# A linear-attention block on one core: the closing's second norm as u*r + w, the last projection in column halves, another order of the closing

## Chip, cores, metric

One core of one Trainium2 chip. The metric is the device time of one execution in microseconds; the median of several executions is compared. "Span" is the time from the first to the last instruction in the profiled execution.

## What is computed

For x of 2 x 4096 x 512 (float32), cut to what the kernel computes:

```python
norm(t) = (t - mean(t)) / sqrt(var(t) + 1e-5)             # over the 512 columns
ffn(t)  = norm(t) * ln_g + ln_b      # what the reference's feed-forward part leaves here
x = x + 0.5 * ffn(norm(x))
x = x + attn(norm(x))
x = x + 0.5 * ffn(norm(x))

def attn(x):                         # 16 heads of 32
    q, k = elu(x @ Wq.T) + 1, elu(x @ Wk.T) + 1
    v = x @ Wv.T
    # for each token t: S += k_t v_t^T ; z += k_t ; out_t = (q_t S) / (q_t . z + 1e-5)
    return out @ Wo.T + bo
```

The kernel writes the two norms of a half step as a gain 1 + rstd * ln_g/2 on x - mean, plus mean, plus ln_b/2. The second half step is what this change touches: with X2 the attention's residual sum, m and r its mean and reciprocal deviation, it is (X2 - m) * (1 + r * gain) + m + shift, where `gain` and `shift` hold half of ln_g and ln_b.

## The kernel before

The 4096 tokens are cut into 32 chunks of 128, and each chunk holds two tiles (batch 0 and 1) of 128 x 512. Weights are turned once at the start and kept as float16 high and low halves; every product of a projection is three passes (high by high, high by low, low by high) over four blocks of 128, so a projection of one tile is 12 matmuls of 512 columns.

Each engine has its own hand-written list of steps, `opening`, `body` and `closing`. The body runs two chunks each time and is software-pipelined: `now` and `prev` are `ops(Step)` objects whose steps act on chunk s (attention), s+1 (projection), s+2 (first norm) and s-1 (`back`, second norm and store). After the loop, `closing` writes out the steps of the last chunks as straight code: `fourth` is chunk 29, `third` 30, `second` 31 and `last` 32, whose `back` steps finish chunk 31. The order between engines comes from semaphores only; within an engine the list's order holds, and a step that waits holds all steps behind it. SyncE issues the transposing transfers (`turn_x`, `turn_k`, `turn_q`, `turn_attn`) in the order of its list.

The steps that the prediction follows, by engine:

- TensorE: `scores` (L1628, the scores of four heads of a chunk into SC), `attend` (L1651, into AV), `update` (L1678, the running state), `project_q`, `project_k`, `project_v` (matmuls at L1595 into PJ), `project_out` (L1690, matmuls at L1700, into PJ).
- VectorE: `mask` (L1165), `split_a` (L1175), `reciprocals` (L1219), `quotient` (L1232), `attn_low` (L1251), `add_out` (L1262: X2 = PJ * out_scale + X1BO), `out_stats` (L1271), `out_mean` (L1282), `back_gain` (L1289: TP = (X2 - m) * TP), `back_y` (L1311: Y = TP + m + shift), and for the last tile of all `back_gain_part` (L1296) and `back_y_part` (L1302) on halves of the columns.
- ScalarE: `copy_scores` (L769), `sums` (L801), `attn_half` (L809), `back_scale` (L700: TP = 1 + r * gain), `back_scale_part` (L667), `store_y` (L660), `store_tile`, `store_part` (L672 and L676).
- GpSimd: `x1_bias` (L432: X1BO = X1 + bo, both tiles), `rstd2_of_x2` (L470 and L472: r for both tiles), `rstd2_of_tile` (L478 and L480), `split_a` (L499), `spread_k`, `spread_q` (L507, L514), `split_s` (L522).
- SyncE: `turn_k` (L309), `turn_q` (L324), `turn_attn` (L335).

At the end of the closing the second norm of a tile therefore goes VectorE (X2, statistics, mean), GpSimd (r), ScalarE (1 + r * gain), VectorE (product, sum), and a store.

## Time and profile before

| | us |
|---|---|
| median of 3 executions | 926.44 (926.18 to 927.87) |
| the profiled execution | 925.02 |
| its span | 923.3 |
| TensorE busy | 892.6 (97%) |
| VectorE busy | 831.2 (90%) |
| ScalarE busy | 754.6 (82%) |
| GpSimd busy | 705.7 (76%) |

Busy times are of the profiled execution. PE is TensorE's matmuls, PEld its weight loads, DVE VectorE, ACT ScalarE, POOL GpSimd, SP SyncE; a q behind a name is the engine's queue of issued transfers. The granted clock of TensorE was 0.996 of full over the span. In a timeline, successive instructions of one kind are merged into one row (x2 is two of them), and matmul rows carry a modelled end, so rows of one engine can overlap by some tenths of a microsecond.

### The profile page before, as it was taken

The page shows a single profiled execution, that of the slowest core. Times are in us where ns is not written, and L with a number is a line of the kernel's source. Part 1 is how long each engine was busy: PE and PEld are TensorE (multiplying, and loading weights), DVE is VectorE, ACT ScalarE, POOL GpSimd, SP SyncE. Part 2 cuts the span into 40 slices and gives each one's busy share as a digit, 9 for nine tenths or more (in the row PEclk, how much of TensorE's full clock was granted, in tenths as well). Part 3 has the DMA queues.
Part 4 walks back from the last instruction along what each step waited for, and adds up shares of the span by engine and source line. Part 5 has one row for each costly group of instructions (what it writes and reads, how often), then busy time and mean ns, then how long its engine had stood idle before and what let it go on. Part 6 is the DMA issues. An engine that isn't in the chain of part 4 may idle for free.

```text
span 923.3 us, 30249 instructions
## 1 busy us (share of the span) xinstructions
PE 892.6 (97%) x10252; PEld 524.5 (57%) x10252; DVE 831.2 (90%) x1537; ACT 754.6 (82%) x1301; POOL 705.7 (76%) x869
## 2 busy tenths in 40 slices
PE   3999999999999999999999999999999999999985
PEld 3555556656555655555665555665555565655562
DVE  7889889999999999999999999999999999999787
ACT  6888888888888888888888888888888888888772
POOL 3369777779777778877778877778977777987772
PEclk9999999999999999999999999999999999999998
DMA  7586797666677766678766668766667766667873
GB/s 250 137 155 131 146 179 159 144 142 150 146 167 159 156 139 148 151 155 165 162 136 153 146 146 182 158 139 146 149 146 171 159 153 142 148 147 160 160 114 94
DMA packets 422090, 140.62 MB, mean 152 GB/s; under 512 B 402608, under 2 KB 402864, under 8 KB 422064
## 3 DMA queue, kind: packets, MB, share of 16 engines
...
q8 instruction: 15, 0.25, 0.1%
q14 instruction: 11, 0.09, 0.1%
...
## 4 chain that ended last, share of the span: by engine, by line
PE 90%; DVE 3%; DMA 2%; issue 2%; SPq 1%; POOL 1%; ACT 1%; DVEq 0%; ACTq 0%; POOLq 0%
PE PJ L1595 51%; PE PJ L1700 16%; PE AV L1674 8%; PE SC L1647 6%; PE AV L1686 5%; PE AV L1671 3%; DMA X<-in_L_attn_x_dram 1%; DMA KS<-KN 1%; SPq L324 1%; DVE AM L1165 0%; DMA AT<-ATTN 0%; PE SC L1572 0%; POOL A L499 0%; DVE TP L1289 0%; DVE wT L1079 0%
## 5 line engine op out<-in xcount | busy, mean ns | idle before, releaser
L1595 PE MATMUL PJ<-wT,XT 128*128 128x512 f16 x2304 | 523.9, 379 | 0.2
L1595 PEld LDWEIGHTS PJ<-wT,XT 128*128 128x128 f16 x2304 | 217.1, 98 | 243.5 <-issue 1.9
L499 POOL TENSOR_TENSOR A<-AM,A 128x512 f16<-128x512 f32 x252 | 288.2, 1163 | 29.1 <-ACT A L782 28.8
L1700 PE MATMUL PJ<-wT,AT 128*128 128x512 f16 x768 | 175.9, 379 | 1.0 <-DMA AT<-ATTN 0.9
L489 POOL TENSOR_SCALAR_AFFINE_SELECT AM<-AM 128x512 f32<-128x512 f32 x124 | 79.2, 639 | 112.9 <-ACT AM L769 112.9
L782 ACT ACTIVATE A<-AM 128x512 f16<-128x512 f32 x256 | 153.9, 632 | 13.9 <-POOL AM L489 10.1
L1674 PE MATMUL AV<-VN,A 128*128 128x33 f16 x3072 | 116.3, 177 | 0.0
L1700 PEld LDWEIGHTS PJ<-wT,AT 128*128 128x128 f16 x768 | 71.2, 97 | 78.1 <-DMA AT<-ATTN 2.1
L1671 PE MATMUL AV<-SS,QS 128*128 128x33 f16 x1024 | 111.7, 178 | 0.0
L1674 PEld LDWEIGHTS AV<-VN,A 128*128 128x128 f16 x3072 | 108.8, 96 | 3.7
L1165 DVE TENSOR_TENSOR AM<-SC,causal 128x512 f32<-128x512 f32 x132 | 90.0, 685 | 19.0 <-PE SC L1647 18.8
L1671 PEld LDWEIGHTS AV<-SS,QS 128*128 128x128 f16 x1024 | 98.0, 96 | 4.0 <-POOL A L499 0.3
L769 ACT ACTIVATE AM<-SC 128x512 f32<-128x512 f32 x124 | 74.1, 598 | 21.8 <-PE SC L1647 21.6
L1647 PE MATMUL SC<-QS,KS 96*128 96x128 f16 x1024 | 83.5, 219 | 4.1 <-issue 2.3
L1647 PEld LDWEIGHTS SC<-QS,KS 96*128 96x128 f16 x1024 | 67.6, 97 | 33.2 <-issue 2.5
L727 ACT ACTIVATE PHI<-PJ,inv_scale 128x512 f32<-128x512 f32 x64 | 43.7, 682 | 44.6 <-PE PJ L1595 44.5
L507 POOL COPY KN<-KN 128x1024 f16<-128x1024 f16 x64 | 66.7, 1043 | 12.5 <-ACT KN L757 12.5
L432 POOL TENSOR_TENSOR X1BO<-X,obias 128x1024 f32<-128x1024 f32 x32 | 75.5, 2359 | 0.0
L522 POOL TENSOR_TENSOR SS<-S,SC_HI 128x528 f16<-128x528 f32 x62 | 73.7, 1189 | 2.0 <-ACT SC_HI L817 1.9
L747 ACT ACTIVATE QN<-PJ,f_scale 128x1024 f16<-128x1024 f32 x64 | 72.1, 1126 | 0.7 <-DVE PJ L1181 0.7
L1125 DVE SCALAR_TENSOR_TENSOR X<-TP,stat,shift 128x512 f32<-128x512 f32 x64 | 47.8, 748 | 19.4 <-POOL X1BO L432 19.3
L1686 PEld LDWEIGHTS AV<-VN,KN 128*128 128x128 f16 x1984 | 58.1, 96 | 7.8 <-DVE TP L1232 0.2
...
## 6 DMA issues: line engine op xcount, KB each, us to landing
...
XT<-XH SPq DMA_TRANSPOSE x64, 3.3
...
```

Source lines behind the costliest of these rows:

```text
L432: g.tensor_tensor(X1BO[:, st.parity(1)], X1[:], obias[:].unsqueeze(1).to_broadcast([P, BATCH, E]), ALU.add).then_inc(x1bo_done.sem, 1)
L489: g.affine_select(out=am, in_=am, compare_op=ALU.is_ge, fill=0.0, base=0, pattern=[[0, QUADS], [1, C]], channel_multiplier=-1).then_inc(sc ...
L499: g.tensor_tensor(A[:, b, LO, hg], AM[:, k % 4], A[:, b, HI, hg], ALU.subtract).then_inc(a_lo.sem, 1)
L769: a.activation(AM[:, k % 4], SC[hg % 2][:], ACT.Copy, scale=SUM_DOWN).then_inc(sc_copied.sem, 1)
L782: a.activation(A[:, b, HI, hg], AM[:, k % 4], ACT.Copy).then_inc(a_hi.sem, 1)
L1165: v.tensor_tensor(AM[:, k % 4].rearrange("p (h q) -> p h q", h=QUADS), SC[hg % 2][:].rearrange("p (h q) -> p h q", h=QUADS), causal[:].uns ...
L1595: ins = t_.matmul(PJ[b], XT[:, w, c, b * C:(b + 1) * C], wT[m_][:, m, c, :], start=(c, w, m) == todo[0], stop=(c, w, m) == todo[-1])
L1647: ins = t_.matmul(SC[hg % 2][:, h * C:(h + 1) * C], KS[cur][0:STACK, head, b * C:(b + 1) * C], QS[cur][0:STACK, head, b * C:(b + 1) * C], ...
L1671: t_.matmul(to, QS[cur][:, head, b * C:(b + 1) * C], SS[:, b, hf, j * DA:(j + 1) * DA], start=True, stop=False)
L1674: ins = t_.matmul(to, A[:, b, w, hg, h * C:(h + 1) * C], VN[cur][:, b, m, head, :], start=False, stop=(w, m) == PASSES[-1])
L1686: ins = t_.matmul(AV2[:, hf, j * DA:(j + 1) * DA], stack, VN[cur][:, b, m, head, :], start=m == HI, stop=m == LO)
L1700: ins = t_.matmul(PJ[b], AT[:, b, w, c * C:(c + 1) * C], wT[3][:, m, c, :], start=(c, w, m) == todo[0], stop=(c, w, m) == todo[-1])
```

## The change

Only code outside the loop's path changes. For chunks 30 and 31 the second half step is computed as u*r + w, with u = (X2 - m) * gain (`gain_u`, VectorE, into TP, reading `gain` from SBUF) and w = X2 + shift. u and r no longer depend on each other. For tiles 0 and 1 of chunk 30 and tile 0 of chunk 31, w is made by GpSimd (`x2_shift`), u*r by ScalarE (`scale_u`), their sum by GpSimd (`sum_y`), and SyncE stores the tile (`store_tile`). For tile 1 of chunk 31, w is made from the projection directly: GpSimd adds shift to X1BO (`x1bo_shift`), VectorE adds the projection (`make_w`, two halves), VectorE makes u*r + w in one instruction (`last_y`), and ScalarE stores the tile whole (`store_last`). r is computed for each tile alone (`rstd2_of_tile`). The last projection, of tile 1 of chunk 31, is done in two halves of 256 columns, the first into PJ[1], the second into SC[0] (`project_out_part`), with its addition and statistics in halves too (`add_out_part`, `out_stats_part`). The parts of the last tile in `back_scale_part`, `back_gain_part`, `back_y_part` and `store_part` are gone.

The order of the closing changes on all engines but SyncE, where only the three stores are added. Left out of the diff below: a new small tile and the new semaphores, conditions in `back_scale` that are no longer needed, and more swaps of neighbouring steps. Of these, ScalarE begins with `sums(0)`, `q_half(0)`, `copy_scores(1, 3)`, `back_scale(1)` of chunk 29 in place of `back_scale(1)`, `copy_scores(1, 3)`, `sums(0)`, `q_half(0)`, and takes `third.copy_scores(1, 3)` ahead of `third.split_a(1, 0)`; VectorE takes `fourth.reciprocals(0)` ahead of `back_y(0)`, `add_s(0)` ahead of `back_gain(1)`, `phi_q(1)` ahead of `back_y(1)`, `low_k(1)` ahead of `low_v(0)`, and for chunk 30 `add_s(0)` ahead of `attn_low(0)` and `quotient(1)` ahead of `second.split_a(0, 1)`; TensorE takes `second.attend(0, 0)` ahead of `second.scores(1, 1)`. The indentation is cut by 16.

```diff
@@ -382,6 +392,9 @@
 second.turn_attn(1)
+second.store_tile(0)
+second.store_tile(1)
+last.store_tile(0)
 
...
@@ -471,13 +484,33 @@
 
+    def x2_shift(b):
+        pool.wait_ge(*x_gained.upto(back, b))
+        pool.wait_ge(*x2_done.upto(back, b))
+        g.tensor_tensor(X[:, st.parity(-1), b], X2[:, b], shift[:], ALU.add).then_inc(x2_shifted.sem, 1)
+
+    def x1bo_shift():
+        pool.wait_ge(*x_gained.upto(s, 1))
+        pool.wait_ge(*x1bo_done.upto(s))
+        g.tensor_tensor(X[:, st.parity(0), 1], X1BO[:, st.parity(0), 1], shift[:], ALU.add).then_inc(x1bo_shifted, 1)
+
     def rstd2_of_tile(b):
-        if b == 0 and st.has(-2):
+        end = back - (steps - 2)
+        if ATTEND:
             pool.wait_ge(*g2_done.upto(st.chunk(-2), 1))
+        else:
+            pool.wait_ge(*u_scaled.upto(0, b))
         pool.wait_ge(*stat2_done.upto(back, b))
-        g.tensor_scalar(var2[:, b:b + 1], stat2[:, b, 1:2], 1.0 + EPS, EPS * EPS, ALU.mult, ALU.add).then_inc(var2_done.sem, 1)
-        pool.wait_ge(*var2_done.upto(back, b))
-        g.tensor_tensor(rstd2[:, b:b + 1], var2[:, b:b + 1], neg_half[:, b:b + 1], ALU.pow).then_inc(rstd2_done.sem, 1)
+        g.tensor_scalar(var2[:, b:b + 1], stat2[:, b, 1:2], 1.0 + EPS, EPS * EPS, ALU.mult, ALU.add).then_inc(var2_tile.sem, 1)
+        pool.wait_ge(*var2_tile.upto(end, b))
+        g.tensor_tensor(rstd2[:, b:b + 1], var2[:, b:b + 1], neg_half[:, b:b + 1], ALU.pow).then_inc(rstd2_tile.sem, 1)
+
+    def sum_y(b):
+        end = back - (steps - 2)
+        pool.wait_ge(*u_scaled.upto(end, b))
+        pool.wait_ge(*x2_shifted.upto(end, b))
+        to = (Y if ATTEND else X1)[:, b]
+        g.tensor_tensor(to, to, X[:, st.parity(-1), b], ALU.add).then_inc(y_summed.sem, 1)
 
...
@@ -576,23 +609,23 @@
 fourth, third, second, last = ops(Step(0, steps - 3)), ops(Step(0, steps - 2)), ops(Step(0, steps - 1)), ops(Step(0, steps))
+fourth.spread_q(0)
 fourth.cut(1, 3)
-fourth.spread_q(0)
 fourth.split_a(1, 1)
...
 fourth.spread_k(1)
+fourth.split_s(0)
 fourth.spread_q(1)
 third.split_a(0, 0)
-fourth.split_s(0)
 third.cut(0, 3)
-fourth.split_s(1)
 third.rstd2_of_x2()
...
 third.split_a(0, 3)
+fourth.split_s(1)
 third.spread_k(0)
...
@@ -609,10 +642,18 @@
 second.split_a(1, 2)
-second.rstd2_of_x2()
 third.x1_bias()
+second.x1bo_shift()
+second.x2_shift(0)
+second.rstd2_of_tile(0)
+second.x2_shift(1)
+second.rstd2_of_tile(1)
+last.x2_shift(0)
+second.sum_y(0)
+second.sum_y(1)
 last.rstd2_of_tile(0)
 last.rstd2_of_tile(1)
+last.sum_y(0)
 
...
@@ -659,21 +700,16 @@
 
-    def back_scale_part(h):
-        half = slice(h * E // 2, (h + 1) * E // 2)
-        act.wait_ge(*rstd2_done.upto(back, 1))
-        act.wait_ge(*attn_lo.upto(back, 1))
-        act.wait_ge(*y_done.upto(st.chunk(-2), 1))
-        a.activation((TP[1], SC[0])[h][:, half], gain[:, half], ACT.Identity, bias=1.0, scale=rstd2[:, 1:2]).then_inc(g2_done.sem, 1)
-
-    def store_part(h):
-        half = slice(h * E // 2, (h + 1) * E // 2)
-        act.wait_ge(*y_done.upto(back, 1 + h))
-        a.dma_start(out[1, bass.ds(back * C, C), half], Y[:, 1, half]).then_inc(y_stored.sem, 16)
-
-    def store_tile(b):
-        act.wait_ge(*y_done.upto(back, b))
-        a.dma_start(out[b, bass.ds(back * C, C), :], Y[:, b]).then_inc(y_stored.sem, 16)
+    def scale_u(b):
+        act.wait_ge(*x2_gained.upto(back, b))
+        act.wait_ge(*rstd2_tile.upto(back - (steps - 2), b))
+        if ATTEND:
+            act.wait_ge(*y_stored.upto(st.chunk(-2)))
+        a.activation((Y if ATTEND else X1)[:, b], TP[b][:], ACT.Copy, scale=rstd2[:, b:b + 1]).then_inc(u_scaled.sem, 1)
+
+    def store_last():
+        act.wait_ge(y_last, 1)
+        a.dma_start(out[1, bass.ds(back * C, C), :], X[:, st.parity(-1), 1]).then_inc(y_stored.sem, 16)
 
...
@@ -945,10 +977,10 @@
 fourth.x_half(1)
+fourth.v_half(1)
 fourth.s_half(0)
-fourth.v_half(1)
+third.split_a(0, 0)
 third.copy_scores(0, 3)
-third.split_a(0, 0)
 third.split_a(0, 1)
...
@@ -991,15 +1023,10 @@
 second.attn_half(1)
-second.back_scale(0)
-second.back_scale(1)
-second.store_y()
-last.back_scale(0)
-last.back_scale_part(0)
-last.back_scale_part(1)
-last.store_tile(0)
-last.store_part(0)
-last.store_part(1)
+second.scale_u(0)
+second.scale_u(1)
+last.scale_u(0)
+last.store_last()
 
...
@@ -1259,6 +1286,8 @@
             dve.wait_ge(*x2_gained.upto(back, b))
+            if not PROJECT:
+                dve.wait_ge(*x2_shifted.upto(0, b))
         v.scalar_tensor_tensor(X2[:, b], PJ[b], out_scale[:], X1BO[:, st.parity(0), b],
...
@@ -1289,18 +1318,46 @@
 
-    def back_gain_part(h):
+    def add_out_part(h):
         half = slice(h * E // 2, (h + 1) * E // 2)
-        dve.wait_ge(*stat2_done.upto(back, 1))
-        dve.wait_ge(*g2_done.upto(back, 1 + h))
-        v.scalar_tensor_tensor((TP[1], SC[0])[h][:, half], X2[:, 1, half], stat2[:, 1, 0:1], (TP[1], SC[0])[h][:, half],
+        dve.wait_ge(*out_filled.upto(s, 1 + h))
+        dve.wait_ge(*x1bo_done.upto(s))
+        dve.wait_ge(*x2_gained.upto(back, 1))
+        dve.wait_ge(*x2_shifted.upto(0, 1))
+        v.scalar_tensor_tensor(X2[:, 1, half], (PJ[1], SC[0])[h][:, half], out_scale[:], X1BO[:, st.parity(0), 1, half],
+                               ALU.mult, ALU.add).then_inc(x2_done.sem, 1)
+
+    def out_stats_part(h):
+        half = slice(h * E // 2, (h + 1) * E // 2)
+        dve.wait_ge(*x2_done.upto(s, 1 + h))
+        v.bn_stats(raw2_part[:, h], X2[:, 1, half]).then_inc(stat2_raw.sem, 1)
+
+    def out_mean_tile(b):
+        dve.wait_ge(*stat2_raw.upto(s, 2 * b))
+        dve.wait_ge(*x2_gained.upto(back, b))
+        dve.wait_ge(*var2_tile.upto(0, b))
+        v.bn_aggr(stat2[:, b], raw2_part[:] if b else raw2[:, 0]).then_inc(stat2_done.sem, 1)
+
+    def gain_u(b):
+        dve.wait_ge(*stat2_done.upto(back, b))
+        if not ATTEND:
+            dve.wait_ge(*u_scaled.upto(0, b))
+        v.scalar_tensor_tensor(TP[b][:], X2[:, b], stat2[:, b, 0:1], gain[:],
                                ALU.subtract, ALU.mult).then_inc(x2_gained.sem, 1)
 
-    def back_y_part(h):
+    def make_w(h):
         half = slice(h * E // 2, (h + 1) * E // 2)
-        dve.wait_ge(*x2_gained.upto(back, 1 + h))
-        v.scalar_tensor_tensor(Y[:, 1, half], (TP[1], SC[0])[h][:, half], stat2[:, 1, 0:1], shift[:, half],
-                               ALU.add, ALU.add).then_inc(y_done.sem, 1)
+        dve.wait_ge(*out_filled.upto(s, 1 + h))
+        dve.wait_ge(x1bo_shifted, 1)
+        at = X[:, st.parity(0), 1, half]
+        v.scalar_tensor_tensor(at, (PJ[1], SC[0])[h][:, half], out_scale[:], at, ALU.mult, ALU.add).then_inc(w_made, 1)
+
+    def last_y():
+        dve.wait_ge(*x2_gained.upto(back, 1))
+        dve.wait_ge(w_made, 2)
+        dve.wait_ge(*rstd2_tile.upto(1, 1))
+        at = X[:, st.parity(-1), 1]
+        v.scalar_tensor_tensor(at, TP[1][:], rstd2[:, 1:2], at, ALU.mult, ALU.add).then_inc(y_last, 1)
 
...
@@ -1521,37 +1578,36 @@
 second.mask(1, 2)
+second.split_a(1, 1)
 second.mask(1, 3)
-second.split_a(1, 1)
 second.reciprocals(0)
...
 second.split_a(1, 3)
+second.attn_low(0)
 third.add_out(0)
-second.attn_low(0)
+third.out_stats(0)
+third.out_mean(0)
 second.reciprocals(1)
 second.quotient(1)
-third.out_stats(0)
+second.gain_u(0)
 second.attn_low(1)
...
 third.out_stats(1)
-third.out_mean(0)
 third.out_mean(1)
-second.back_gain(0)
-second.back_gain(1)
-second.back_y(0)
-second.back_y(1)
+second.gain_u(1)
 second.add_out(0)
 second.out_stats(0)
-second.add_out(1)
-second.out_mean(0)
-second.out_stats(1)
-second.out_mean(1)
-last.back_gain(0)
-last.back_gain_part(0)
-last.back_gain_part(1)
-last.back_y(0)
-last.back_y_part(0)
-last.back_y_part(1)
+second.out_mean_tile(0)
+second.add_out_part(0)
+second.out_stats_part(0)
+last.gain_u(0)
+second.add_out_part(1)
+second.out_stats_part(1)
+second.out_mean_tile(1)
+last.gain_u(1)
+second.make_w(0)
+second.make_w(1)
+last.last_y()
 
...
@@ -1698,6 +1754,16 @@
             ins = t_.matmul(PJ[b], AT[:, b, w, c * C:(c + 1) * C], wT[3][:, m, c, :],
+                            start=(c, w, m) == todo[0], stop=(c, w, m) == todo[-1])
+        ins.then_inc(out_filled.sem, 1)
+
+    def project_out_part(b, h):
+        half = slice(h * E // 2, (h + 1) * E // 2)
+        pe.wait_ge(*attn_turned[b].upto(s))
+        pe.wait_ge(*x2_done.upto(back, b))
+        todo = [(c, w, m) for c in range(GROUPS) for w, m in PASSES]
+        for c, w, m in todo:
+            ins = t_.matmul((PJ[1], SC[0])[h][:, half], AT[:, b, w, c * C:(c + 1) * C], wT[3][:, m, c, half],
                             start=(c, w, m) == todo[0], stop=(c, w, m) == todo[-1])
...
@@ -1779,8 +1845,8 @@
 fourth, third, second = ops(Step(0, steps - 3)), ops(Step(0, steps - 2)), ops(Step(0, steps - 1))
+fourth.attend(0, 1)
 fourth.scores(1, 3)
-fourth.attend(0, 1)
 fourth.project_q(1)
...
@@ -1793,9 +1859,9 @@
 third.scores(0, 2)
-third.scores(0, 3)
 fourth.project_out(0)
 fourth.project_out(1)
+third.scores(0, 3)
 third.project_k(0)
...
@@ -1829,7 +1895,8 @@
 second.project_out(0)
-second.project_out(1)
+second.project_out_part(1, 0)
+second.project_out_part(1, 1)
 
```

## Rows read from the trace of the kernel before

**Rows 1.** the page's busy line: busy us, share of span, instructions

```profile
PE 892.6 (97%) x10252; PEld 524.5 (57%) x10252; DVE 831.2 (90%) x1537; ACT 754.6 (82%) x1301; POOL 705.7 (76%) x869
```

**Rows 2.** busy time of each engine in stretches of the end, us (instructions)

```profile
core 0: us, PE busy (x) PEld busy (x) DVE busy (x) ACT busy (x) POOL busy (x), PEclk, DMA share, GB/s
907.80:913.20 5.40, 5.37 (x24) 2.17 (x24) 3.29 (x8) 1.30 (x2) 3.21 (x3) 1.00 0.25 49
913.20:923.30 10.10, 0.00 (x0) 0.00 (x0) 6.47 (x13) 1.56 (x3) 1.51 (x4) 0.60 0.28 104
```

**Rows 3.** timeline of TensorE: start us, us, operation, count [idle before <-releaser]

```profile
866.31 0.40 PE L1647 MATMUL SC<-QS,KS 96*128 96x128 f16 x4 [0.54 <-ACT AM L769]
...
880.23 0.62 PE L1647 MATMUL SC<-QS,KS 96*128 96x128 f16 x8 [0.57 <-DMA KS<-KN]
...
904.39 2.75 PE L1700 MATMUL PJ<-wT,AT 128*128 128x512 f16 x12
907.79 5.38 PE L1700 MATMUL PJ<-wT,AT 128*128 128x512 f16 x24 [0.65 <-DMA AT<-ATTN]
```

**Rows 4.** timeline of VectorE (DVE), from 901 us to its end

```profile
901.04 0.68 DVE L1175 TENSOR_TENSOR A<-AM,A 128x512 f16<-128x512 f32 x1
...
901.92 0.70 DVE L1232 TENSOR_TENSOR SC<-AV,RDEN 128x512 f32<-128x512 f32 x1
...
903.87 0.68 DVE L1251 SCALAR_TENSOR_TENSOR ATTN<-SC,ATTN 128x512 f16<-128x512 f32 x1
...
906.54 0.69 DVE L1251 SCALAR_TENSOR_TENSOR ATTN<-SC,ATTN 128x512 f16<-128x512 f32 x1
...
911.00 1.41 DVE L1289 SCALAR_TENSOR_TENSOR TP<-X,stat,TP 128x512 f32<-128x512 f32 x2 [2.00 <-ACT TP L700]
...
913.64 0.74 DVE L1262 SCALAR_TENSOR_TENSOR X<-PJ,out_scale,X1BO 128x512 f32<-128x512 f32 x1
...
916.65 0.18 DVE L1282 BATCH_NORM_AGGREGATE stat<-raw 128x2 f32<-128x6 f32 x1 [0.16 <-DVE raw L1271]
...
918.79 0.49 DVE L1296 SCALAR_TENSOR_TENSOR SC<-X,stat,SC 128x256 f32<-128x256 f32 x1
...
920.24 0.48 DVE L1302 SCALAR_TENSOR_TENSOR Y<-SC,stat,shift 128x256 f32<-128x256 f32 x1
```

**Rows 5.** timelines of ScalarE (ACT; ACTq are its issued transfers) and GpSimd (POOL)

```profile
901.50 1.24 POOL L499 TENSOR_TENSOR A<-AM,A 128x512 f16<-128x512 f32 x1 [0.86 <-ACT A L782]
...
905.91 0.60 ACT L809 ACTIVATE ATTN<-SC 128x512 f16<-128x512 f32 x1 [1.05 <-DVE SC L1232]
...
910.12 2.36 POOL L432 TENSOR_TENSOR X1BO<-X,obias 128x1024 f32<-128x1024 f32 x1
...
916.29 0.56 POOL L480 TENSOR_TENSOR rstd<-var,neg_half 128x1 f32<-128x1 f32 x1
...
920.35 0.95 ACTq L672 DMA_DIRECT2D out_dram<-Y  x2
```

**Rows 6.** transfers: us to landing (900:908); GB/s in 40 slices (919:924)

```profile
AT<-ATTN SPq DMA_TRANSPOSE x2, 3.1
...
GB/s 0 0 0 0 0 0 0 0 0 0 0 0 0 0 115 410 344 360 426 369 320 320 344 353 336 360 140 0 0 0 0 0 0 0 0 0 0 0 0 0
```

**Rows 7.** GpSimd's, SyncE's, ScalarE's issues; landing at 872, in loop; GB/s 872 to 882

```profile
867.99 0.62 POOL L514 COPY QN<-QN 128x512 f16<-128x512 f16 x1
...
871.72 4.41 SPq L309 DMA_TRANSPOSE KS<-KN  x1
...
871.95 0.41 ACTq L660 DMA_DIRECT2D out_dram<-Y  x1
...
KS<-KN SPq DMA_TRANSPOSE x1, 8.5
...
KS<-KN SPq DMA_TRANSPOSE x2, 4.4
...
GB/s 222 216 211 168 236 325 426 401 385 352 174 171 247 219 232 207 211 220 228 222 220 11 0 0 5 8 0 0 0 0 0 0 0 0 0 0 0 0 0 22
```

More of the change, by code:

```diff
@@ L141, in build @@
         raw2 = sb("raw2", [P, BATCH, 6])
+        raw2_part = sb("raw2_part", [P, 2, 6])
         wsq = AM
@@ L205, in build @@
         y_stored = sig("y_stored", 1, 16, 16)
+        x2_shifted, u_scaled, y_summed = sig("x2_shifted", 2), sig("u_scaled", 2), sig("y_summed", 2)
+        x1bo_shifted, w_made = sem("x1bo_shifted"), sem("w_made")
+        var2_tile, rstd2_tile, y_last = sig("var2_tile", 2), sig("rstd2_tile", 2), sem("y_last")
         steps = CHUNKS
@@ L336, in turn_attn, with store_tile @@
                                                ATTN[:, b].rearrange("p f e -> p (f e)")).then_inc(attn_turned[b].sem, 16)
+                    def store_tile(b):
+                        sp.wait_ge(*y_summed.upto(back - (steps - 2), b))
+                        sp.dma_start(out[b, bass.ds(back * C, C), :], (Y if ATTEND else X1)[:, b]).then_inc(y_stored.sem, 16)
                 return Ops
@@ L368, in closing @@
             def closing():
-                fourth, third, second = ops(Step(0, steps - 3)), ops(Step(0, steps - 2)), ops(Step(0, steps - 1))
+                fourth, third, second, last = ops(Step(0, steps - 3)), ops(Step(0, steps - 2)), ops(Step(0, steps - 1)), ops(Step(0, steps))
                 fourth.turn_q(0)
@@ L690, in back_scale @@
                             return
-                        act.wait_ge(*rstd2_done.upto(back, 0 if ATTEND else b))
+                        act.wait_ge(*rstd2_done.upto(back))
                         if FRONT:
                             act.wait_ge(*x1_done.upto(f, b))
-                        elif PROJECT:
+                        else:
                             act.wait_ge(*x_lo.upto(n, b))
-                        else:
-                            act.wait_ge(*attn_lo.upto(back, b))
-                            if not ATTEND:
-                                act.wait_ge(*y_done.upto(st.chunk(-2), b))
                         a.activation(TP[b][:], gain[:], ACT.Identity, bias=1.0, scale=rstd2[:, b:b + 1]).then_inc(g2_done.sem, 1)
@@ L928, in closing @@
                 fourth, third, second, last = ops(Step(0, steps - 3)), ops(Step(0, steps - 2)), ops(Step(0, steps - 1)), ops(Step(0, steps))
-                fourth.back_scale(1)
-                fourth.copy_scores(1, 3)
                 fourth.sums(0)
                 fourth.q_half(0)
+                fourth.copy_scores(1, 3)
+                fourth.back_scale(1)
                 fourth.split_a(1, 1)
@@ L966, in closing @@
                 third.q_half(0)
+                third.copy_scores(1, 3)
                 third.split_a(1, 0)
                 third.split_a(1, 1)
-                third.copy_scores(1, 3)
                 third.attn_half(0)
@@ L1461, in closing @@
                 fourth, third, second, last = ops(Step(0, steps - 3)), ops(Step(0, steps - 2)), ops(Step(0, steps - 1)), ops(Step(0, steps))
+                fourth.reciprocals(0)
                 fourth.back_y(0)
-                fourth.reciprocals(0)
                 fourth.quotient(0)
@@ L1466, in closing @@
                 fourth.low_q(0)
+                fourth.add_s(0)
                 fourth.back_gain(1)
-                fourth.add_s(0)
                 fourth.front_mean1(1)
+                fourth.phi_q(1)
                 fourth.back_y(1)
-                fourth.phi_q(1)
                 fourth.attn_low(0)
@@ L1477, in closing @@
                 fourth.attn_low(1)
+                fourth.low_k(1)
                 fourth.low_v(0)
-                fourth.low_k(1)
                 fourth.x_low(0)
@@ L1503, in closing @@
                 third.mask(1, 2)
+                third.add_s(0)
                 third.attn_low(0)
-                third.add_s(0)
                 third.phi_q(1)
@@ L1513, in closing @@
                 third.reciprocals(1)
+                third.quotient(1)
                 second.split_a(0, 1)
-                third.quotient(1)
                 second.split_a(0, 3)
@@ L1821, in closing @@
                 second.scores(1, 0)
+                second.attend(0, 0)
                 second.scores(1, 1)
-                second.attend(0, 0)
                 second.scores(1, 2)
```

## The prediction

> **What bounds the kernel now.** I read the page's busy line first: TensorE is busy 892.6 of 923.3 us [rows 1]. The table by windows then says where it is not. In the last 10.10 us it has no instruction at all [rows 2], and VectorE works 6.47 us of them. So the end is a chain after the last projection. I read it off the timelines from the back. The last matmuls run from 907.79 for 5.38 us, to 913.17 [rows 3]. VectorE, though, adds the output of tile 0 only at 913.64, because from 911.00 it was busy with the second norm of chunk 30, which had waited 2.00 us for ScalarE's scaled gain [rows 4]. Then come statistics, mean, GpSimd's power, ScalarE's scaled gain, the product and the sum, the last of them at 920.24 for 0.48, to 920.72 [rows 4]. The last store is issued at 920.35 for 0.95 [rows 5]. The transfer view of the last 5 us has bytes moving in slices 14 to 26 of 0.128 us, from 920.8 to 922.4, at some 350 GB/s [rows 6]; the span ends 0.9 us later.
>
> Earlier in the closing, TensorE's gaps are small: 0.54 at 866.31 on ScalarE's copy, 0.57 at 880.23 on the transpose of KS [rows 3]. That transpose matters most: issued at 871.72, it landed after 8.5 us, where the same one in the loop lands in 4.4 [rows 7]. All that follows hangs on it, so nothing gained on TensorE ahead of 880.23 counts unless KS lands earlier too.
>
> **The change, part by part.** Nothing changes in the loop, whose code is the same. I cost the closing from 854 on.
>
> 1. *Reordering before 880.* On TensorE scores(0,3) goes behind the two output projections, which removes the 0.54 at 866.31; I book nothing, as KS then makes it wait 0.57 + 0.54 instead of 0.57. On GpSimd split_s(0) goes ahead of spread_q(1). That copy ran at 867.99 for 0.62 [rows 7]; behind a split of 1.2 us it ends some 1.1 later, near 869.75. SyncE's turn_q(1) waits for it, and turn_k(1), which brings KS, is queued behind turn_q(1) on SyncE. The turns had lost some time to the queue already, so I take 0.5 us for turn_q(1), and between 0 and 0.5 for KS, since the transfer engines are full there and a late issue partly hides. On ScalarE store_y of chunk 28, issued 0.2 us after KS [rows 7], comes about 2 us later; the engines move its 512 KB in the same stretch all the same. Value taken: +0.3. Bounds: -1.1 (KS lands before TensorE is ready, that is 0.57 + 0.54) and +4.1 (it is held once more by 8.5 - 4.4).
>
> 2. *Scores, masks and the last quotients, 897 to 903.* On TensorE attend(0,0) goes ahead of scores(1,1); on VectorE split_a(1,1), now at 901.04 because it waits for ScalarE's half, goes ahead of mask(1,3). So mask(1,3) starts when that split ends, not before it, and quotient(0), at 901.92 now [rows 4], moves to about 902.4. attn_low(0), now ahead of add_out(0), starts near 903.7 where it started at 903.87 [rows 4]. Its transpose lands 3.1 us after issue [rows 6], so project_out(0) begins at 907.65, not 907.79: -0.1.
>
> 3. *What stands before attn_low(1).* The first three operations of chunk 30's norm, and gain_u(0), now come ahead of attn_low(1), which started at 906.54 [rows 4]. Consecutive VectorE instructions follow each other by 0.66 (two of them in 1.41 [rows 4]); a mean waits 0.16 for its statistics [rows 4]. From 904.35: add_out(0) 0.66, statistics and mean 1.1, reciprocal 0.25, quotient(1) from 906.35 to 907.05, ScalarE's half 0.60 [rows 5] with gain_u(0) under it, attn_low(1) from 907.7 to 908.4. Its transpose lands 3.1 later, at 911.5, where it came in time for 910.4 before. TensorE waits over 1 us for it (it has nothing else left), and the last projection runs 911.55 to 914.3, against 913.17: +1.15. Who waits: VectorE's two half additions, all else being ahead of them.
>
> 4. *The last projection in halves.* 24 matmuls of 256 columns for 12 of 512. The trace has none of this shape. Bounds: half the time each (no cost), or the 379 ns recorded for every matmul now, which would add up to the 2.6 us of a projection again; consecutive projections take 5.38 for two [rows 3], so the columns fill the time, and I take no cost. The first half is there at 913.0.
>
> 5. *The tail on VectorE.* Gone are ScalarE's scaled gain ahead of the product, and the two back_y of chunk 30 (1.4 us) from VectorE; they go to GpSimd (x2_shift, sum_y) and ScalarE (scale_u). VectorE has: add_out(1), statistics, mean and gain_u(1) of chunk 30 from 908.35 to 910.85; add_out(0) to 911.5; statistics and mean of it to 912.65; first half added at 913.05; its statistics to 914.0; last gain_u(0) to 914.65; second half, whose matmuls ended at 914.3, added to 915.1; its statistics to 915.6; mean at 915.95; gain_u(1) 916.0 to 916.65; make_w twice at 0.40 (halves run 0.49, and the next follows by 0.4 [rows 4]) to 917.55; last_y 917.6 to 918.35. The rstd that last_y needs is ready at 917.0 (0.19 and 0.56 on GpSimd [rows 5]), hidden under gain_u(1) and make_w; without that cover it would cost all of 0.9. The end of the arithmetic is 918.35 for 920.72: -2.37.
>
> 6. *GpSimd as the second path.* A pass of 128x512 with two inputs is half of the 2.36 us of a 128x1024 one [rows 5], 1.18. It now has x1_bias (started at once, at 902.75), x1bo_shift, x2_shift three times, two or three sums. By my schedule its last rstd is ready at 917.0, and last.sum_y(0) ends at 918.2, level with last_y. Bounds: no effect, and 1.2 us if one more pass slips ahead; I take 0.1.
>
> 7. *Stores.* The two last stores of 256 KB each are issued together at 918.3 (SyncE and ScalarE), while now the first goes out at 919.96 and its bytes start at 920.8. 512 KB take the 1.6 us of [rows 6]. So bytes move from 919.15 to 920.75, and the span ends 0.9 later at 921.65: the 2.37 shrinks to 1.65, because two full tiles go out at once.
>
> 8. *Two inputs from SBUF.* gain_u reads X2 and gain from SBUF, where back_gain read PSUM for one of them. The nearest row is split_a on VectorE: at 901.04 it takes 0.68 while GpSimd begins a 1.24 us instruction at 901.50 [rows 4, 5]. They overlap by 0.2 us, and GpSimd's is about 0.08 longer than its usual 1.16. I take 0.15 for the encounters on the path; bound 1.6 (below). The Trainium skill, SBUF — State Buffer, section Who interferes with whom, says that VectorE with two SBUF inputs and a reading GpSimd instruction exclude each other, the later one blocked for the whole instruction. That overlap speaks against a full block.
>
> Sum on the span: -1.65 + 0.3 + 0.15 + 0.1 = about -1.1, so 922.2. The profiled execution took 925.02 and the median of the runs is 926.44, 1.4 more; I carry the difference over: 926.44 - 1.1 = 925.3.
>
> **Rivals.**
> - *KS lands earlier.* In its 8.5 us there are nearly 3, from 877.4 to 880.2, in which almost no bytes moved [rows 7], so bandwidth is not all of it; if the new timing escapes it, TensorE starts at once and all behind moves by 1.1 instead of -0.3. Then -1.1 - 0.3 - 1.1 = -2.5: 923.9. For it: the loop's 4.4. Against: the same queue order.
> - *VectorE and GpSimd exclude each other* whenever gain_u meets a pass: chunk 30's gain_u(0) meets x2_shift(0) (0.55 us, and attn_low(1) with it), the last gain_u(0) meets the sums (1.05). -1.1 - 0.15 + 1.6 = +0.35: 926.8. The one overlap in the trace is against it. The rule of the Trainium skill named in part 8 would give this.
> - *KS is held once more* (the slower side). turn_q(1) is late, KS's descriptors queue behind it, and store_y now falls into the middle. Price 8.5 - 4.4 = 4.1, of which 0.3 is booked: -1.1 + 3.8 = +2.7, 929.1. It decides when KS takes over 11.4 us to land.
> - *The change doesn't act.* If sum_y and stores, not VectorE, end the kernel, with GpSimd 1.2 us late: -1.1 + 1.1 = 0, 926.4.
>
> **How the numbers follow.** Forecast 0.50 (its own range 924.3 to 926.3), earlier KS 0.25, exclusion 0.10, no effect 0.07, KS held 0.08. 0.2% is 1.85 us, about what a measurement of this kernel can tell from nothing. Faster by more than that (below 924.6): the earlier KS and a quarter of the forecast's spread, 0.38. Slower by more (over 928.3): 0.09. Between: 0.53. The range reaches from the earlier KS with 0.7 to spare, 923.2, to just over exclusion, 927.3.
>
> **What would show it.** Right: the last projection begins near 911.5, about 1.1 us after project_out(0) ends; last_y ends near 918.4; the two last stores start together; KS lands 8 to 9 us after issue; gain_u takes about 0.75 beside GpSimd. Wrong: a project_out_part ending well before 914 (then the transpose of ATTN was not what it waited for), halves of projection over 1.4 us, gain_u over 1 us, or last_y waiting for GpSimd.

## The result

The changed kernel took 928.20 us (median of 20 runs, 926.06 to 930.44), the kernel before in the same series 925.96 (20 runs, 923.81 to 927.87). The ratio is 1.0026, with a 95% interval of 1.0018 to 1.0035: some 2.4 us slower, where 1.1 less was forecast. The profiled execution took 927.47, its span 925.7.

Both kernels vary by some 4 us from execution to execution, and part of that lies ahead of the closing: in the profile of after, the loop already ends 1.20 us later than in that of before, and the loop's code is the same. So profiles are compared here from one landmark: the start of chunk 30's first scores (the pair of score groups that TensorE starts at 861.54 in the profile of before, at 862.74 in after's). "From the landmark" below is always that. Before needed 61.76 us from there to the end of the span, after 62.96. The single profile shows 1.20 us of the 2.4 in the closing, then; it can't show where the rest of the medians' difference lies.

**TensorE, timeline of after** (columns as in [rows 3], to be held against them):

```profile
866.98 5.34 PE L1756 MATMUL PJ<-wT,AT 128*128 128x512 f16 x24
...
881.20 0.62 PE L1703 MATMUL SC<-QS,KS 96*128 96x128 f16 x8 [0.88 <-DMA KS<-KN]
...
901.26 3.90 PE L1756 MATMUL PJ<-wT,AT 128*128 128x512 f16 x12
...
907.52 5.66 PE L1756 MATMUL PJ<-wT,AT 128*128 128x512 f16 x24
914.49 1.48 PE L1766 MATMUL PJ<-wT,AT 128*128 128x256 f16 x12 [1.31 <-DMA AT<-ATTN]
915.81 1.47 PE L1766 MATMUL SC<-wT,AT 128*128 128x256 f16 x12
```

The wait of 0.54 for ScalarE's copy is gone, as foreseen. KS is waited for 0.88, where 1.11 and more was foreseen; KS landed 8.0 us after its issue. The last projection is in its halves; the second starts 1.32 after the first, so 24 matmuls of 256 columns cost what 12 of 512 do. It had to wait 1.31 for the transpose of ATTN.

**VectorE, timeline of after** (held against [rows 4]):

```profile
901.90 0.69 DVE L1202 TENSOR_TENSOR A<-AM,A 128x512 f16<-128x512 f32 x1
...
903.39 0.70 DVE L1259 TENSOR_TENSOR SC<-AV,RDEN 128x512 f32<-128x512 f32 x1
904.00 2.60 DVE L1202 TENSOR_TENSOR A<-AM,A 128x512 f16<-128x512 f32 x1
906.53 0.68 DVE L1278 SCALAR_TENSOR_TENSOR ATTN<-SC,ATTN 128x512 f16<-128x512 f32 x1
...
913.04 0.87 DVE L1345 SCALAR_TENSOR_TENSOR TP<-X,stat,gain 128x512 f32<-128x512 f32 x1
...
916.88 0.88 DVE L1345 SCALAR_TENSOR_TENSOR TP<-X,stat,gain 128x512 f32<-128x512 f32 x1
...
919.94 0.47 DVE L1353 SCALAR_TENSOR_TENSOR X<-SC,out_scale,X 128x256 f32<-128x256 f32 x1
921.36 0.75 DVE L1360 SCALAR_TENSOR_TENSOR X<-TP,rstd,X 128x512 f32<-128x512 f32 x1 [0.94 <-POOL rstd L506]
```

Two rows are new. The second split_a (L1202; L1175 before) took 2.60 us, where before the same step took 0.76. And last_y (L1360) stood 0.94 us idle for GpSimd's rstd.

**GpSimd, timeline of after** (held against [rows 5]):

```profile
902.59 1.16 POOL L532 TENSOR_TENSOR A<-AM,A 128x512 f16<-128x512 f32 x1 [1.09 <-ACT A L814]
903.70 2.35 POOL L445 TENSOR_TENSOR X1BO<-X,obias 128x1024 f32<-128x1024 f32 x1
906.20 1.53 POOL L495 TENSOR_TENSOR X<-X1BO,shift 128x512 f32<-128x512 f32 x1
...
915.93 2.94 POOL L513 TENSOR_TENSOR Y<-Y,X 128x512 f32<-128x512 f32 x2
918.95 0.73 POOL L504 TENSOR_SCALAR var<-stat 128x1 f32<-128x1 f32 x1
919.76 0.55 POOL L506 TENSOR_TENSOR rstd<-var,neg_half 128x1 f32<-128x1 f32 x1
...
921.19 1.26 POOL L513 TENSOR_TENSOR X<-X 128x512 f32<-128x512 f32 x1
```

x1_bias (L445) ran from 903.70 to 906.05. VectorE's split_a began at 904.00 and ended at 906.60, 0.55 us after GpSimd was through; alone it takes 0.68. Both its inputs, AM and A, lie in SBUF. The tiny power chain (L504, L506) of the last chunk stood behind two sum_y. The last arithmetic of all is not last_y, which ends at 922.11, but GpSimd's last sum_y, which ends at 922.45; its store is the last to be issued.

The last two stores and their bytes (40 slices of 0.175 us from 919; held against [rows 6]):

```profile
922.14 0.35 ACTq L712 DMA_DIRECT2D out_dram<-X  x1
...
922.48 0.33 SPq L346 DMA_DIRECT2D out_dram<-X  x1
...
GB/s 0 0 0 0 257 374 374 398 94 0 0 0 0 0 0 0 0 0 0 0 0 0 70 351 386 386 375 375 374 386 293 0 0 0 0 0 0 0 0 0
```

The bytes of both tiles move from 922.9 to 924.4, at 350 to 390 GB/s. From the end of last_y to the end of the span it is 3.59 us, from the end of GpSimd's last sum_y 3.25; from the last sum of before it was 2.58 [rows 4].

### The profile page after: what moved, and what is told of

The parts are those of the page before. It is cut to its first block, busy times and chain, and to the rows that moved or that the text cites. A ratio compares the mean times of both kernels' runs of the same rounds, so it can differ in the third digit from the quotient of the medians.

```text
span 925.7 us, 30286 instructions
## 1 busy us (share of the span) xinstructions
PE 895.2 (97%) x10264; PEld 526.6 (57%) x10264; DVE 833.8 (90%) x1536; ACT 753.5 (81%) x1299; POOL 715.9 (77%) x878
## 4 chain that ended last, share of the span: by engine, by line
PE 89%; DVE 3%; DMA 3%; issue 2%; POOL 1%; SPq 1%; ACT 1%; POOLq 0%; DVEq 0%; ACTq 0%
PE PJ L1651 51%; PE PJ L1756 16%; PE AV L1730 8%; PE SC L1703 6%; PE AV L1742 5%; PE AV L1727 3%; DMA KS<-KN 1%; DMA X<-in_L_attn_x_dram 1%; DMA shift<-in_L_ffn_ln_b_dram 1%; SPq L330 1%; DVE AM L1192 0%; PE SC L1628 0%; DMA AT<-ATTN 0%; POOL A L532 0%; POOL Y L513 0%
## 5 line engine op out<-in xcount | busy, mean ns | idle before, releaser
L445 POOL TENSOR_TENSOR X1BO<-X,obias 128x1024 f32<-128x1024 f32 x32 | 75.4, 2357 | 0.0
L833 ACT ACTIVATE DEN<-AV,den_eps 128x16 f32<-128x16 f32 x64 | 17.7, 276 | 55.9 <-PE AV L1730 55.8
```

Source lines behind the costliest of these rows:

```text
L445: g.tensor_tensor(X1BO[:, st.parity(1)], X1[:], obias[:].unsqueeze(1).to_broadcast([P, BATCH, E]), ALU.add).then_inc(x1bo_done.sem, 1)
```

## The experiments

Theory A, formed on these rows: VectorE and GpSimd keep each other out when VectorE reads two inputs from SBUF and GpSimd reads SBUF, and the swaps moved split_a(1,3) of chunk 31 right behind the start of x1_bias, which the new tail had moved forward. Theory B: the new order and the late turn of ATTN themselves make the closing longer.

**The landmarks of all profiles**, us from the landmark (by subtraction, good to 0.05; the time of split_a(1,3) is its duration, "scores" the start of chunk 31's scores(1,0), "arithmetic" the end of VectorE's last instruction). Each ratio is to runs of the kernel before in the same series; there are four series (changed; e1 to e4; e5 to e8; e9, e10 and changed again), not all on one chip, so ratios of different series are compared by their intervals. The column "scores to end" leaves out what comes ahead of the last scores, a slower clock there too, and is the steadiest measure of the tail: kernels that do the same there agree within 0.06.

| kernel | KS landed, TensorE starts | scores | split_a(1,3) starts, takes | arithmetic | span ends | scores to end | ratio to before (95%) |
|---|---|---|---|---|---|---|---|
| before | 18.69 | 36.08 | 40.99, 0.76 | 59.18 | 61.76 | 25.68 | 1 |
| changed | 18.46 | 35.75 | 41.26, 2.60 | 59.37 | 62.96 | 27.21 | 1.0026 (1.0018 to 1.0035) |
| changed, again | 19.17 | 36.58 | 42.08, 2.69 | 60.29 | 63.81 | 27.23 | 1.0015 (1.0002 to 1.0028) |
| e1_bias_early | 19.03 | 36.86 | 42.46, 1.43 | 59.39 | 63.00 | 26.14 | 1.0002 (0.9987 to 1.0017) |
| e2_bias_moved | 18.76 | 36.08 | 40.98, 0.76 | 59.16 | 61.74 | 25.66 | 0.9995 (0.9981 to 1.0009) |
| e3_norm_only | 18.76 | 35.37 | 40.28, 0.76 | 57.26 | 60.85 | 25.48 | 0.9987 (0.9976 to 0.9997) |
| e4_swaps_only | 19.68 | 36.35 | 41.77, 0.68 | 59.95 | 62.51 | 26.16 | 1.0017 (1.0002 to 1.0033) |
| e5_swaps_and_bias | 19.33 | 36.01 | 41.43, 2.69 | 63.05 | 65.58 | 29.57 | 1.0032 (1.0020 to 1.0043) |
| e6_gain_psum | 18.84 | 35.35 | 40.25, 0.76 | 55.61 | 59.15 | 23.80 | 0.9976 (0.9966 to 0.9985) |
| e7_no_lock | 18.86 | 35.53 | 40.44, 0.76 | 55.82 | 59.11 | 23.58 | 0.9975 (0.9964 to 0.9985) |
| e8_early_swaps | 18.74 | 35.91 | 40.81, 0.76 | 59.01 | 61.53 | 25.62 | 0.9999 (0.9989 to 1.0008) |
| e9_change_no_lock | 19.43 | 36.09 | 41.51, 0.68 | 56.88 | 60.43 | 24.34 | 0.9982 (0.9970 to 0.9994) |
| e10_turn_first | 18.60 | 35.10 | 40.16, 0.76 | 55.38 | 58.94 | 23.84 | 0.9980 (0.9970 to 0.9991) |

**e1_bias_early**: the changed kernel with one line moved.

```diff
 third.spread_q(1)
+third.x1_bias()
 second.split_a(0, 0)
...
 second.split_a(1, 2)
-third.x1_bias()
 second.x1bo_shift()
```

> The changed kernel with x1_bias of chunk 30 moved on GpSimd from behind split_a(1,2) of chunk 31 to ahead of split_a(0,0) of chunk 31, where GpSimd stood idle 2.07 us. Theory A (GpSimd's 2.35 us pass over SBUF locked out VectorE's split_a(1,3), whose inputs are both in SBUF and which took 2.60 us in place of 0.68): split_a(1,3) takes 0.7 again, attn_low(0), the turn of ATTN and all behind come 1.8 us earlier, 926.3 us. Theory B (the closing is longer because of the order of VectorE's steps and the wait for the second turn of ATTN, and the long split_a only filled idle time): split_a may shorten, but the time stays at 928.0.

Measured: 927.18 against 926.92, ratio 1.0002, which is 0.0024 below the changed kernel's 1.0026, and 0.0013 below its repetition, where the intervals overlap. split_a(1,3) still took 1.43, because now x1bo_shift ran beside its start. VectorE's step, then GpSimd's:

```profile
905.46 1.43 DVE L1202 TENSOR_TENSOR A<-AM,A 128x512 f16<-128x512 f32 x1
...
905.07 1.27 POOL L495 TENSOR_TENSOR X<-X1BO,shift 128x512 f32<-128x512 f32 x1
```

GpSimd's pass ends at 906.34, VectorE's step 0.55 later. The 0.7 expected of split_a was missed, the reason for it bears theory A out. The span of this profile did not fall (63.00 for 62.96), because its last scores came 1.1 us later from the landmark; from the scores to the end it is 26.14 for 27.21, and split_a(1,3) is 1.17 shorter. B would have left that stretch as it was.

**e2_bias_moved**: the kernel before, the same pass early.

```diff
 second.split_a(1, 2)
+third.x1_bias()
 second.rstd2_of_x2()
-third.x1_bias()
```

> The kernel before with one line moved: x1_bias of chunk 30 ahead of rstd2_of_x2 of chunk 31, so that it starts right behind split_a(1,2) at 902.7 as in the changed kernel. There VectorE's split_a(1,3) starts at 902.5, ahead of it. Theory A (whoever starts first holds the port, the other waits): split_a(1,3) stays at 0.7 to 0.8, x1_bias takes 2.6 to 3.0 in place of 2.36, the time stays at 926.0 (within 0.5). Theory B' (the two slow each other down evenly, whoever is first): split_a(1,3) takes 1.3 or more, and the time grows by 0.6 to 2.

Measured: ratio 0.9995 and split_a(1,3) 0.76, so no price: in this order VectorE comes first, at 906.34, and it is x1_bias that takes 2.81 for 2.36, as expected. An early x1_bias is harmless by itself.

```profile
906.52 2.81 POOL L432 TENSOR_TENSOR X1BO<-X,obias 128x1024 f32<-128x1024 f32 x1
```

**e3_norm_only** and **e4_swaps_only** part the change in two: e3 is the changed kernel with the swaps ahead of 903 us undone on four engines, e4 the kernel before with these swaps made. A few of the lines, as in e4:

```diff
-second.mask(1, 3)
 second.split_a(1, 1)
+second.mask(1, 3)
...
-second.scores(1, 1)
 second.attend(0, 0)
+second.scores(1, 1)
```

> The changed kernel with all swaps ahead of 903 us undone on the four engines: only the new form of the norm, the halves, and the order of the tail are left, x1_bias still behind split_a(1,2). Theory A: split_a(1,3) starts ahead of x1_bias, as in the kernel before, so it takes 0.8 and x1_bias the longer; the time is about 926.5. Theory B (the tail itself is longer): 928.2, as the changed kernel.

> The kernel before with only the swaps ahead of 903 us made: old norm, old projection, old tail. Theory A: in the changed kernel the transposes of KS and QS landed 0.3 to 0.5 earlier against the loop's end than before, and without an early x1_bias nothing collides: 925.7 (0.3 less than before). Rival (the swaps cost the time): 927.5 to 928.

Measured: 0.9987 for the norm alone (0.5 us slower than before was expected, it was 1.2 faster) and 1.0017 for the swaps alone (0.3 faster was expected). Multiplied they give 1.0004. The whole change gave 1.0026, and 1.0015 when repeated, so by the times 0.0022 or 0.0011 (2.0 or 1.0 us) belong to neither part but to their meeting; the interval of the product alone is about 0.0019 to either side. The traces are sharper. From the scores to the end the swaps add 0.48 and the norm takes off 0.20, but both together add 1.53 and 1.55: 1.3 us for the meeting. Only where both are there did split_a(1,3) take 2.60 - 0.68 = 1.9 us too long; on the other side, the four gain_u lose less there than in e3 (below). In e3, VectorE comes first at x1_bias, and GpSimd is the one that waits; later it is now one, now the other. VectorE of e3, then its GpSimd:

```profile
903.53 0.76 DVE L1202 TENSOR_TENSOR A<-AM,A 128x512 f16<-128x512 f32 x1
...
910.84 1.48 DVE L1345 SCALAR_TENSOR_TENSOR TP<-X,stat,gain 128x512 f32<-128x512 f32 x1
...
914.77 1.39 DVE L1345 SCALAR_TENSOR_TENSOR TP<-X,stat,gain 128x512 f32<-128x512 f32 x1
...
903.70 2.81 POOL L445 TENSOR_TENSOR X1BO<-X,obias 128x1024 f32<-128x1024 f32 x1
...
907.89 1.71 POOL L490 TENSOR_TENSOR X<-X,shift 128x512 f32<-128x512 f32 x1
...
910.49 1.26 POOL L490 TENSOR_TENSOR X<-X,shift 128x512 f32<-128x512 f32 x1
```

x1_bias takes 2.81 for 2.35, as split_a(1,3) was under way. gain_u at 910.84 waits for the pass of 910.49 to end at 911.75 and is through at 912.32. The four gain_u of e3 took 0.87, 1.48, 1.39 and 0.76; less 0.75 each, 1.5 us. The exclusion rival had priced them at 1.6. In the changed kernel they took 0.75, 0.87, 0.88 and 0.76, only 0.26 us too long: with VectorE late by split_a(1,3), most of those encounters didn't come about.

**e5_swaps_and_bias**: e4 with the line of e2 moved; old norm and old tail.

> The kernel before with the swaps ahead of 903 us and with x1_bias of chunk 30 ahead of rstd2_of_x2 of chunk 31: old norm, whole last projection, old tail. The swaps bring VectorE's split_a(1,3) behind the start of x1_bias (in e4_swaps_only it starts 1.32 us after GpSimd's last split_a begins, that is 0.2 after x1_bias would). Theory A (exclusion, first come first served): split_a(1,3) takes 2.3 to 2.6 us, and the kernel is 1.7 to 2 us slower than e4_swaps_only, a ratio of about 1.0037 to the kernel before. Theory B (the interaction of swaps and new tail lies elsewhere): split_a(1,3) 0.7 to 0.9, ratio 1.0017 as e4_swaps_only.

```profile
905.15 2.69 DVE L1175 TENSOR_TENSOR A<-AM,A 128x512 f16<-128x512 f32 x1
...
904.95 2.35 POOL L432 TENSOR_TENSOR X1BO<-X,obias 128x1024 f32<-128x1024 f32 x1
```

0.20 us behind, VectorE waits for the whole pass. One line costs nothing in e2 (0.9995) and, with the swaps, raises 1.0017 to 1.0032: some 1.4 us, with intervals that touch, and 3.1 us of span in the profiles, of which a part belongs to a slower clock: TensorE's granted clock was 0.66 of full over 909 to 914, 24 matmuls of a projection took 7.03 us there for 5.50 in e4, and VectorE waited 1.64 us for them. So the collision was made again with the old norm and the old tail.

**e6_gain_psum**: e3 with gain filled into TP by ScalarE, which was idle.

```diff
+def fill_gain(b):
+    act.wait_ge(*(attn_lo.upto(back, b) if ATTEND else u_scaled.upto(0, b)))
+    a.activation(TP[b][:], gain[:], ACT.Copy).then_inc(gain_filled.sem, 1)
...
-v.scalar_tensor_tensor(TP[b][:], X2[:, b], stat2[:, b, 0:1], gain[:],
+v.scalar_tensor_tensor(TP[b][:], X2[:, b], stat2[:, b, 0:1], TP[b][:],
```

(The wait is written shorter than it stands; gain_u also waits for gain_filled.)

> e3_norm_only (new norm and tail, old order ahead of 903 us) with ScalarE, idle there, filling TP[b] with gain, so that gain_u reads one input from PSUM and works in place. Theory A (the locks come from gain_u's second input in SBUF): its four instructions take 0.75 us each in place of 0.87, 1.48, 1.39 and 0.76, x2_shift of tile 0 takes 1.27 in place of 1.71. VectorE is ready for last_y 1.3 us sooner, but last_y waits for GpSimd's rstd, whose queue gets shorter by about 0.5 only: ratio to e3 about 0.9995, and last_y's wait grows from 0.94 to 1.7 or more. Rival (gain_u is slow for another reason, or VectorE alone bounds the tail): durations unchanged, or a full 1.3 us less.

```profile
906.09 0.74 DVE L1358 SCALAR_TENSOR_TENSOR TP<-X,stat,TP 128x512 f32<-128x512 f32 x1
...
909.29 0.76 DVE L1358 SCALAR_TENSOR_TENSOR TP<-X,stat,TP 128x512 f32<-128x512 f32 x1
...
913.12 0.74 DVE L1358 SCALAR_TENSOR_TENSOR TP<-X,stat,TP 128x512 f32<-128x512 f32 x1
...
906.36 1.27 POOL L491 TENSOR_TENSOR X<-X,shift 128x512 f32<-128x512 f32 x1
...
912.07 2.50 POOL L514 TENSOR_TENSOR Y<-Y,X 128x512 f32<-128x512 f32 x2
```

Every gain_u takes 0.74 to 0.76, beside passes of GpSimd that now take 1.27 and 1.25 each. VectorE's arithmetic ends 1.65 us earlier from the landmark than in e3, and last_y waits for nothing: GpSimd had lost more to the lock than was expected of it, so that its queue came free earlier too. From the scores to the end it is 23.80 for 25.48. Ratio 0.9976, against 0.9987 of e3 in another series, with intervals that overlap; the kernel before is beaten clear of noise. The expectation of a growing wait was wrong.

**e7_no_lock**: e6 with x1_bias as in e1 and sum_y(0) of chunk 30 ahead of x2_shift(1).

> e6_gain_psum with GpSimd's queue reordered: x1_bias of chunk 30 ahead of split_a(0,0) of chunk 31, and sum_y(0) of chunk 30 ahead of x2_shift(1), so that one pass less stands ahead of the last rstd. Theory A (after the locks the tail is bound by GpSimd's queue): the wait of last_y for rstd falls under 0.3 us, the kernel is 2 to 2.5 us faster than e3_norm_only, a ratio of 0.996 to the kernel before. Rival (VectorE or the turn of ATTN bounds the tail): at most 0.7 us less than e6.

Measured: 0.9975, VectorE's arithmetic at 55.82 for 55.61. Missed, the rival holds: in e6 GpSimd's last sum_y ends 0.25 us after last_y, in e7 0.19 before it. GpSimd's queue was the last path by that little, and moving its passes could buy no more than the two tenths by which the stretch from the scores is shorter.

**e8_early_swaps**: e4 without the two late swaps shown above.

> e4_swaps_only with its two late swaps undone (attend(0,0) against scores(1,1) on TensorE, split_a(1,1) against mask(1,3) on VectorE): only the swaps ahead of 897 us are left. If the cost of the swaps lies in the later landing of QS and KS: ratio 1.0010 to 1.0017, QS landing in 6.1 us where it takes 4.4. If it lies in the masks, which delay split_a(1,3) by 0.5 us against the last scores: ratio 1.0000 to 1.0005, and split_a(1,3) starts 4.9 us after scores(1,0) as in the kernel before.

Measured: 0.9999. split_a(1,3) starts 4.90 after the scores, as before (4.91); with the late swaps it is 5.42 to 5.60 in six profiles. From the scores to the end e8 is 25.62, as before (25.68), and e4 26.16: what the swaps cost there is all of the late ones. The times say the same less sharply: intervals of e4 and e8 overlap a little. QS did land in 6.1 us here too, and the kernel is not slower for it.

**e9_change_no_lock**: the changed kernel whole, with e6's fill, x1_bias as in e1 and x1bo_shift behind rstd2_of_tile(0).

> The changed kernel whole, swaps included, with the three encounters of VectorE and GpSimd taken away: gain filled into TP by ScalarE for gain_u, x1_bias of chunk 30 ahead of split_a(0,0) of chunk 31, x1bo_shift behind rstd2_of_tile(0). Theory A (the change was slower by its locks): split_a(1,3) 0.7 us, every gain_u 0.75 us, and 3 to 3.5 us less than the changed kernel: a ratio of 0.999 to the kernel before (0.9976 of e6 plus what the swaps cost). Rival (the swaps alone make it slow, in any company): 1.001 or more.

Measured: 925.32 against 926.37, ratio 0.9982 (interval below 1), and:

```profile
906.18 0.68 DVE L1214 TENSOR_TENSOR A<-AM,A 128x512 f16<-128x512 f32 x1
```

The change as given is slower than before, and is faster than before once its engines no longer meet. In the same series the changed kernel stands at 1.0015: the step is 0.0033, some 3 us. The traces say 2.9: from the scores to the end 24.34, where the changed kernel takes 27.21 and 27.23.

**e10_turn_first**: e7 with attn_low(1) earlier.

```diff
 third.add_out(0)
-third.out_stats(0)
-third.out_mean(0)
 second.reciprocals(1)
 second.quotient(1)
-second.gain_u(0)
+third.out_stats(0)
 second.attn_low(1)
+third.out_mean(0)
+second.gain_u(0)
```

> e7_no_lock with VectorE's reciprocals(1), quotient(1) and attn_low(1) of chunk 31 taken ahead of chunk 30's mean and gain_u(0), so that the second turn of ATTN is issued earlier. In e7 VectorE waited 0.61 us for the first half of the last projection, TensorE 1.35 for that turn. If the turn is the last bound of the tail: attn_low(1) 0.7 to 0.8 us earlier, VectorE's wait gone, 0.6 us less than e7, a ratio of 0.9968. If VectorE's own work bounds it: the wait moves elsewhere, 0.9975 as e7.

Measured: 0.9980, the same as e7 within the intervals. attn_low(1) starts 3.26 after attn_low(0) in place of 4.09, VectorE's wait of 0.61 for the projection is gone, and last_y waits 0.51 for rstd instead; GpSimd's last sum_y again ends last, 0.35 us after last_y. The turn of ATTN alone is not what bounds the tail; what it would give with a shorter queue on GpSimd was not run.

**e11_change_again**: the changed kernel once more.

> The changed kernel as it is, beside the two others on the same chip. Theory A: split_a(1,3) takes 2.4 to 2.7 us again, last_y waits about 0.9 for GpSimd's rstd, ratio 1.0026. Rival (the 2.60 us of the one profile was an accident of that execution): split_a(1,3) 0.7 to 1.0.

```profile
905.67 2.69 DVE L1202 TENSOR_TENSOR A<-AM,A 128x512 f16<-128x512 f32 x1
...
923.13 0.75 DVE L1360 SCALAR_TENSOR_TENSOR X<-TP,rstd,X 128x512 f32<-128x512 f32 x1 [0.94 <-POOL rstd L506]
```

The same two rows: the 2.60 was no accident. The ratio is 1.0015 (1.0002 to 1.0028), less than in the first series and less than the 1.0026 expected, with intervals that overlap.

## Why the prediction was wrong

**Part 8 failed, and with it the sum.** It booked 0.15 us for all encounters of VectorE and GpSimd, from one overlap of 0.2 us in [rows 4, 5], which it read as speaking against a full block. It speaks for a full block: VectorE's split_a was there first, 0.46 us ahead, and GpSimd's instruction ended 1.02 us after it, 0.14 less than the 1.16 it takes alone. The encounters of passes of 512 columns and more all have this form: the second ends its usual time less 0.12 to 0.20 after the first (split_a 0.55 after, of 0.68; gain_u 0.55 to 0.57 after, of 0.75; x1_bias 2.22 after, of 2.35), as if that little had been done before the wait. A full block therefore leaves just such a short overlap in the trace. The 1.24, 2.81 and 1.71 of GpSimd and the 2.60, 1.48 and 1.39 of VectorE (1.24 is of before, 2.60 of the changed kernel, the rest of e3) are one thing seen from both sides. The Trainium skill, SBUF — State Buffer, section Who interferes with whom, gives just this pair, VectorE with two SBUF inputs against a GpSimd instruction that reads SBUF, as a conflict over an exclusive lock in which the order of issue decides who blocks; this case's traces agree, with 2.60 and 2.69 us for 0.68 while a 2.35 us pass ran. By weighing it at gain_u alone, I had the rule as a rival at 926.8 with a chance of 0.10, and its price there, 1.6, was nearly right for e3 (1.5) and far too high for the changed kernel (0.26): it had the rule right and the place of the loss wrong. What no rival held is the larger encounter, of a step that the change doesn't touch (split_a, L1175) with one that it only moves (x1_bias, L432): part 6 says of x1_bias no more than "started at once, at 902.75". A step moved to 902.75 had to be held against VectorE's list from 902.75 on, where split_a(1,3) stands with both inputs in SBUF. The prediction had both times in hand: by part 2 quotient(0) moves to 902.4, and split_a(1,3) behind it starts near 903.0, a quarter of a microsecond into the pass. Without the encounters the same change needs 2.9 us less from the scores to the end (e9); 0.15 was booked for them.

**Part 2 had the cause of the collision and didn't follow it.** In the traces with the late swaps, split_a(1,3) starts 0.5 later against the scores (5.42 and more for 4.91): attend(0,0) ahead of scores(1,1) delays mask(1,1), and mask(1,3) then waits for split_a(1,1). I had mask(1,3) and quotient(0) later by 0.5, and let the new place of attn_low(0), ahead of add_out(0), take it back. Where nothing collides that holds: in e9 attn_low(0) starts 6.18 after the scores, before 6.25, in place of the 0.17 earlier that was said. In the changed kernel it is 8.04. The 0.5 is what put split_a(1,3) behind the start of x1_bias, and that consequence was not drawn.

**Part 6 was sized wrong.** 0.1 us was booked for GpSimd's queue; last_y waited 0.94 for it in four profiles, and in the changed kernel GpSimd's last sum_y ends 0.34 us after last_y and ends the kernel. Its passes were longer than 1.18 (1.27, and 2.94 for two when blocked), and one of its var steps took 0.73 for 0.19. Free of locks (e6) the wait is gone, and the last sum_y ends 0.25 after last_y.

**Right** were: the later landing of KS on average (booked +0.3; without the early swaps TensorE starts 18.60 to 18.86 from the landmark, with them 18.46 to 19.68, their mean 0.4 more), though in the one profile of the changed kernel it starts 0.23 earlier; the turn of ATTN that TensorE waits for (over 1 us said, 1.31 measured), though the kernel gained nothing when it came earlier (e10); the halves without cost (part 4); the two stores going out together (part 7: 3.3 us from the later of the two last sums to the end said, 3.25 measured). Part 5 said 2.37 us less of arithmetic; counted from the scores to the end of VectorE's arithmetic, before took 23.10, e9 20.79: 2.31 less where nothing collides. So the tail was costed well for a kernel whose engines don't meet, and e9 is that kernel. That the forecast of -1.1 us is also what the new norm gives without the swaps (0.9987, 1.2 us) is chance: e3 has 1.5 us of encounters in it, and its last scores start 0.7 us earlier from the landmark than before's, which nothing in the forecast stands for.

**Held against the measured +2.4 us** (1.0026; 1.4 by 1.0015): the two parts alone measure +1.6 (1.0017) and -1.2 (0.9987), which leaves 2.0 or 1.0 for their meeting, uncertain by some 2 us to either side. In the traces, from the scores to the end, it is +0.48, -0.20 and 1.3 for the meeting. That 1.3 is 1.9 for split_a(1,3), less 1.2 that gain_u loses in e3 and not here, and the rest, 0.6, isn't broken down. The slower side that I had named, KS held once more, did not occur in any of the 13 profiles (TensorE starts at 19.68 at most).

**Open.** In four of the profiles with the late swaps TensorE's granted clock fell for a few microseconds in the closing: in the changed kernel to a mean of 0.72 of full over 898 to 903, when repeated to 0.83 over 882 to 892, in e1 to 0.83 over 883 to 893 and 0.78 over 898 to 904, in e5 to 0.66 over 909 to 914. e4 and e9, with the same swaps, and all seven profiles without them kept 1.00 there. TensorE had been waiting now and again in the 20 us ahead (0.88, 1.03 and 1.22 us in the changed kernel), but in before too (0.57, 1.28, 1.06). Whether the swaps bring the falls on isn't settled. In the changed kernel a projection takes 3.90 us for 2.75 by it, yet this fall doesn't explain the result: when repeated, the clock was 1.00 over 893 to 905, the projection took 2.75, and the scores-to-end stretch was the same (27.23 for 27.21). How the late swaps' 0.5 us in the trace becomes a measured 1.6 us (interval 0.2 to 3.1), and why the last scores start at 35.10 to 35.53 in e3, e6, e7 and e10 where before and e2 have 36.08, is open as well.
